# Weights that are loaded as they lie in HBM and turned by DMA transposes, in a cross-attention and ternary-FFN kernel

## The chip, the cores and the metric

The kernel runs on one core of a Trainium2 chip. The metric is the device time of one execution in microseconds (us). The core has TensorE (PE in the profile; its weight loads are PEld), VectorE (DVE), ScalarE (ACT), GpSimd (POOL) and SyncE (SP), which issues nearly all DMAs here. PEclk is the TensorE clock that the throttle granted.

## The reference

There are B = 4 sequences of L = 512 rows, D = 512, context width C = 256, head width H = 128, hidden width F = 2048.

```python
query = ctx @ Wq.T + bq;  key = ctx @ Wk.T + bk          # ctx (4,512,256) -> (4,512,128)
attention = softmax(query @ key.T)                       # (4,512,512)
x = x + layernorm(x) @ attention
scale = max(mean(|w|), 1e-8); wq = clip(round(w / scale), -1, 1)   # for w1 (2048,512) and w2 (512,2048)
x = x + gelu(layernorm(x) @ w1q.T + b1) @ w2q.T + b2
```

The scale of a weight matrix is the mean of its absolute values. So no weight can be rounded until the whole matrix has been loaded and summed, and w1 must be rounded before the first hidden matmul, w2 before the first output matmul.

## The kernel before

All operands of the large matmuls are f16. Activations are carried as a high and a low f16 half, ternary weights are exact in f16. P = 128, NT = ND = 4 tiles of rows or of D, NF = 16 tiles of F, NCH = 8 chunks of 1024 columns per weight matrix.

**Order of the work.** Every engine has its own hand-written program, and semaphores tie them. Per sequence b there are: projection and scores (f32), exponentials, `attend` (layernormed x times attention, 4 tiles of 12 matmuls), the second layernorm, `hidden(b, g)` (4 groups of 32 matmuls), `output(b, t)` (4 tiles of 32 matmuls). PE does attend(0) and attend(1) first, then hidden(0, 0) to hidden(0, 3) with the projection of sequence 2 before the last, scores of sequence 2, and output(0, 0) to output(0, 3). From then on FFN and attention of later sequences alternate.

**The weights.** SP loads each weight matrix in two halves, a half in four DMAs of 512 KB, each to 32 partitions (`load_w`, L257), so that four 32-row blocks of a matrix's transpose lie in the four partition groups. ACT sums the absolute values chunk by chunk (`sum_abs`, L688), the last two chunks of w2 are summed by DVE (L837). PE's `total` (L470) adds over partitions, and DVE makes the scale and its inverse (`quantiser_scale`, L850). POOL multiplies and rounds each chunk in two instructions (`round_weights`, L393: L397 and L400). DVE clips (L886) and transposes 32x32 blocks of pairs of f16 as u32 (L893) into `w1T` or `w2T`. PE waits for `turned_done`, one per chunk.

**The interleaving by pairs.** Since u32 pairs are turned, feature order inside a tile is permuted: `w1T[..., s]` is read with a stride of 2, results are written through `e_rows` and `e_columns`, and POOL writes `x2n` (L375) in blocks of 32.

**x2T, the layernormed x of the FFN.** For sequence 0 its tiles 0 and 1, and then 2 and 3, are normalised by POOL (`layernorm2`, L356), split in a high half by ACT (L671) and a low half by DVE (L783), staged in `gT_lo`, and turned by four DMA transposes of 128x1024 f16 (`turn_first_x2`, L274). They stand in SP's queue behind 12 of the 16 weight loads. hidden(0, 0) waits for all four. Later sequences use DMA transposes of 128x2048 f16.

**Buffers.** `w2T` lies over the lower half of `w1_raw`, the stages of later sequences over the upper half and over `w2_raw`.

The functions that the diff touches, and what calls them:

## Time and profile before

| | us |
|---|---|
| median of 3 runs | 320.81 (319.93 to 322.96) |
| the profiled execution | 320.93 |
| its span | 319.1 |
| PE busy | 304.6 |
| DVE / ACT / POOL busy | 166.8 / 144.0 / 117.4 |

Read the slices first: the busy share of PE in 40 slices of 8 us shows where it was not full. Then read the chain of work that ended last in order of time, which says from which moment on nothing but PE counts, and the timelines of the engines ahead of that moment. The mean of one f16 matmul of 512 columns is shown as about 380 ns, but matmuls are pipelined: 32 of them take 6.91 us in the chain, 0.216 us each. Idle time of an engine other than PE costs nothing by itself.

### The profile page before, as it was taken

The numbers are of one execution on the slowest core, as the hardware profiler recorded it, in microseconds if no ns is written. First come the engines' busy times: TensorE is split into PE (matmuls) and PEld (weight loads), VectorE is DVE, ScalarE is ACT, GpSimd is POOL, SyncE is SP. The second block draws the span as 40 slices with busy tenths as digits, with TensorE's granted clock in tenths as the row PEclk, the third lists the DMA queues.
The fourth block names the chain that finished last, engine by engine and source line by source line (L and its number), as shares of the span: only waits on it lengthen the run. The fifth ranks groups of instructions, "written<-read, shape, count | busy, mean of one in ns | idle before, by whom it ended". The sixth has DMA issues, their size and how long they took to land.

```text
span 319.1 us, 3686 instructions
## 1 busy us (share of the span) xinstructions
PE 304.6 (95%) x1397; PEld 143.7 (45%) x1397; DVE 166.8 (52%) x295; ACT 144.0 (45%) x251; POOL 117.4 (37%) x129
## 2 busy tenths in 40 slices
PE   7999979969987999999999999999999999999995
PEld 3465534434433444444444444444444444444455
DVE  2788868898689881754425630553424103342101
ACT  2287776686450652455374332456350006772000
POOL 0385369938998993000460560000470000000000
PEclk9999999999999999999999999999999999999999
DMA  8999999992100499000003947000016110000011
GB/s 198 271 209 211 213 137 219 214 278 68 31 0 0 87 175 267 0 2 0 0 0 69 174 89 199 0 0 0 2 31 130 39 66 0 0 2 0 33 62 40
DMA packets 57922, 28.04 MB, mean 88 GB/s; under 512 B 42800, under 2 KB 51760, under 8 KB 57904
## 3 DMA queue, kind: packets, MB, share of 16 engines
q1 hardware_dynamic: 57536, 27.53, 40.9%
q10 hardware_dynamic: 368, 0.27, 0.3%
q8 instruction: 11, 0.18, 0.2%
q14 instruction: 7, 0.06, 0.1%
HBM read 15.21 MB, written 4.19 MB: 61 GB/s over the span
## 4 chain that ended last, share of the span: by engine, by line
PE 73%; DMA 8%; SPq 8%; DVE 6%; ACT 3%; issue 2%
PE ps_e L526 31%; PE ps_t L509 29%; DMA w_raw<-in_L_ffn_w 7%; PE ps_e L494 6%; SPq L260 6%; PE ps_e L435 2%; PE ps_e L533 2%; PE ps_e L443 2%; ACT abs_out L695 1%; DVE tern L886 1%; DMA ctx_sb<-in_ctx 1%; SPq L277 1%; SPq L252 1%; DVE gT_lo L899 1%; DVE ctxT L763 1%
## 5 line engine op out<-in xcount | busy, mean ns | idle before, releaser
L509 PE MATMUL ps_t<-x2T,w1T 128*128 128x512 f16 x512 | 112.5, 379 | 0.0
L526 PE MATMUL ps_e<-w_raw,gT_hi 128*128 128x512 f16 x240 | 91.1, 380 | 3.0 <-DVE w_raw L893 3.0
L526 PE MATMUL ps_e<-w_raw,gT_lo 128*128 128x512 f16 x240 | 91.1, 380 | 0.0
L703 ACT ACTIVATE ps_t<-ps_t,b_col 128x512 f32<-128x512 f32 x64 | 42.2, 663 | 94.4 <-PE ps_t L509 94.4
L899 DVE SCALAR_TENSOR_TENSOR gT_lo<-ps_t,h_scale,gT_hi 128x512 f16<-128x512 f32 x64 | 44.9, 743 | 64.6 <-ACT gT_hi L708 64.6
L509 PEld LDWEIGHTS ps_t<-x2T,w1T 128*128 128x128 f16 x512 | 50.1, 98 | 60.6 <-issue 0.7
L905 DVE SCALAR_TENSOR_TENSOR x_sb<-ps_e,h_unscale,x_sb 128x512 f32<-128x512 f32 x15 | 11.2, 747 | 57.5 <-PE ps_e L526 57.5
L708 ACT ACTIVATE gT_hi<-ps_t,h_scale 128x512 f16<-128x512 f32 x64 | 40.3, 685 | 0.0
L526 PEld LDWEIGHTS ps_e<-w_raw,gT_hi 128*128 128x128 f16 x240 | 23.4, 98 | 33.1 <-DVE w_raw L893 4.5
L526 PEld LDWEIGHTS ps_e<-w_raw,gT_lo 128*128 128x128 f16 x240 | 23.5, 98 | 29.0 <-issue 1.7
L363 POOL TENSOR_SCALAR var_eps<-mv 128x4 f32<-128x4 f32 (+1 forms) x5 | 1.0, 196 | 81.4 <-DVE mv L835 81.4
L400 POOL TENSOR_SCALAR w_raw<-w_raw 128x1024 f16<-128x1024 f32 x16 | 22.0, 1378 | 1.4
L651 ACT ACTIVATE probs<-ps_e,row_max 128x512 f32<-128x512 f32 x16 | 10.9, 686 | 25.9 <-DVE row_max L803 25.7
L397 POOL TENSOR_SCALAR w_raw<-w_raw,inv_scale 128x1024 f32<-128x1024 f32 x16 | 19.5, 1218 | 6.3 <-DVE inv_scale L855 6.3
L494 PE MATMUL ps_e<-w_raw 128*128 128x512 f16 x96 | 21.7, 380 | 0.0
L391 POOL TENSOR_TENSOR x_sb<-x_sb,b_sb 128x512 f32<-128x512 f32 x16 | 21.2, 1357 | 0.0
L383 POOL TENSOR_SCALAR probs<-probs,row_inv 128x512 f32<-128x512 f32 x16 | 14.7, 935 | 15.6 <-DVE row_inv L808 15.6
L695 ACT ACTIVATE abs_out<-w_raw 128x1024 uint8<-128x1024 f32 x14 | 14.9, 1061 | 5.5 <-DMA w_raw<-in_L_ffn_w 5.2
L443 PE MATMUL ps_e<-qkT 128*128 128x512 f32 x32 | 14.8, 596 | 0.7 <-ACT qkT L645 0.7
L353 POOL TENSOR_SCALAR xn<-x_sb,neg_mean,rstd 128x512 f32<-128x512 f32 x16 | 14.9, 945 | 0.4
L494 PEld LDWEIGHTS ps_e<-w_raw 128*128 128x128 f16 x96 | 9.4, 98 | 11.3
L886 DVE TENSOR_SCALAR tern<-w_raw 128x1024 f16<-128x1024 f16 x16 | 14.1, 879 | 0.6 <-POOL w_raw L400 0.6
(90 smaller groups left out, 276.6 us busy)
## 6 DMA issues: line engine op xcount, KB each, us to landing
w_raw<-in_L_ffn_w SPq DMA_DIRECT2D x16, 512.0 KB, 10.0
x_sb<-in_x SPq DMA_DIRECT2D x4, 1024.0 KB, 8.2
out<-x_sb SPq DMA_DIRECT2D x15, 256.0 KB, 2.5
ctx_sb<-in_ctx SPq DMA_DIRECT2D x16, 128.0 KB, 3.4
b_sb<-in_L_ffn_b SPq DMA_DIRECT2D x1, 256.0 KB, 8.6
out<-x_sb SPq DMA_DIRECT2D x2, 128.0 KB, 2.3
x2n<-in_L_xattn_Wq ACTq DMA_DIRECT2D x1, 128.0 KB, 2.9
x2n<-in_L_xattn_Wk ACTq DMA_DIRECT2D x1, 128.0 KB, 3.8
```

The lines of the kernel that those rows point to most:

```text
L260: sp.dma_start(raws[m][q * R:(q + 1) * R, h * n:(h + 1) * n, :], w_views[m][q, :, h * n:(h + 1) * n, :]).then_inc(w_here[m][h], 16)
L391: nc.gpsimd.tensor_tensor(x_sb[:, b, t], x_sb[:, b, t], b2_sb[:], ALU.add).then_inc(b2_added, 1)
L397: nc.gpsimd.tensor_scalar(src, src, inv_scale[:, m:m + 1], ROUND, ALU.mult, ALU.add).then_inc(scaled, 1)
L400: nc.gpsimd.tensor_scalar(chunk_whole(m, c).rearrange("p n (i s) -> p n s i", s=2), src, -ROUND, 1.0, ALU.add, ALU.mult).then_inc(rounded, 1)
L443: nc.tensor.matmul(attn_bank(b, t)[:], qkT[:, 0, t * P:(t + 1) * P], qkT[:, 1], start=True, stop=True).then_inc(scores_ready, 1)
L494: mm = nc.tensor.matmul(attn_bank(b, t)[:], xnT(b)[:, u, j, t * P:(t + 1) * P], probsT(b)[:, v, j], start=(n == 0 and j == 0), stop=(n == ...
L509: mm = nc.tensor.matmul(ps_t[t][:], w1T[:, k // 2, j, :, k % 2], x2T[:, b % 2, v, :, j], start=(v == 0 and j == 0), stop=(v == 1 and j == ...
L526: mm = nc.tensor.matmul(y_bank(t)[:], part[:, k, t * P:(t + 1) * P], w2T[:, k], start=(k == 0 and part is gT_hi), stop=(k == NF - 1 and pa ...
L695: nc.scalar.activation(abs_out[:], flat[:, c * CH:(c + 1) * CH], ACT.Abs, accum_out=abs_sum[:, m, c:c + 1]).then_inc(abs_done, 1)
L703: nc.scalar.activation(ps_t[t][:], ps_t[t][:], ACT.Gelu, scale=1.0 / LN_SCALE, bias=b1_col[:, k:k + 1]).then_inc(gelu_done, 1)
L708: nc.scalar.activation(gT_hi[:, k], ps_t[t][:], ACT.Identity, scale=h_scale[:, 0:1]).then_inc(gT_hi_done, 1)
L899: nc.vector.scalar_tensor_tensor(out=gT_lo[:, k], in0=ps_t[t][:], scalar=h_scale[:, 0:1], in1=gT_hi[:, k], op0=ALU.mult, op1=ALU.subtract) ...
```

## The change

1. **Loads.** Each weight matrix is loaded over 128 partitions in four DMAs of 1 MB, w1 as 128 partitions x 4 rows of 512 (rows of 2 KB), w2 as 128 rows of 2048 (8 KB). SP issues all 16 loads (w2's second half, the context of sequence 2, b2, x of sequences 2 and 3 too) ahead of the first transposes.
2. **Turning.** DVE only clips. w1 is clipped in place and turned by eight DMA transposes of 128x1024 f16 (`turn_w1`). w2's chunks are clipped into `w2_ternary`, four chunks of room over the upper half of `w1_raw`, and turned two at a time by four DMA transposes of 128x2048 (`turn_w2`). All stand in SP's queue, turn_w1(0) between the two pairs of x2T. PE waits for `w1T_here[c]` and `w2T_here[n]`. The first clip of w2 waits until w1's chunks 4 to 7 have been turned, its fifth and seventh for the first and second turn of w2.
3. **Order.** All absolute sums go to ACT, earlier; the w1 total moves ahead of attend(1) on PE and on DVE, the w2 total from behind hidden(0, 1) to behind hidden(0, 0). The small layernorm steps (variance plus epsilon, minus mean) move from POOL to DVE, as does the normalisation of tiles 2 and 3 of sequence 0. POOL starts rounding w1 before it makes the `rstd2` that this needs.
4. **Plain order.** The pair interleaving goes, with `e_rows`, `e_columns` and the blocked write of x2n.

The core of the diff (what is left out renames semaphores, warms up on another tile, and makes views plain):

```diff
-        w1_raw = sb("w1_raw", [P, F // R, P])
-        w2_raw = sb("w2_raw", [P, D // R, F // Q])
-        w1T = sb("w1T", [P, NF // 2, ND, P, 2], F16)
+        w1_raw = sb("w1_raw", [P, NF, D])
+        w2_raw = sb("w2_raw", [P, ND, F])
+        w1T = sb("w1T", [P, NF, ND, P], F16)
...
-        tern = sb("tern", [P, 2, CH], F16)
...
+        w2_ternary = w1_stage[:, 0].rearrange("p v m -> p (v m)").rearrange("p (n c) -> p n c", c=CH)
+        N_TERNARY = 4
...
         def chunk_source(m, c):
 
             if m == 0:
-                return w1_raw[:].rearrange("p (q k) e -> p q k e", q=Q)[:, :, 2 * c:2 * c + 2]
-            return w2_raw[:, :, 2 * R * c:2 * R * (c + 1)].rearrange("p (s h) i -> p h s i", s=2)
+                return w1_flat[:, c * CH:(c + 1) * CH]
+            return w2_raw[:, :, 2 * P * c:2 * P * (c + 1)]
 
         def chunk_whole(m, c):
 
-            return chunk_source(m, c)[:, :, 0].bitcast(F16)
-
-        def chunk_turned(m, c):
+            src = chunk_source(m, c)
             if m == 0:
-                return w1T[:, c].rearrange("p j f s -> p (j f s)").bitcast(U32).rearrange(
-                    "p (j q r) -> p q j r", j=ND, q=Q)
-            return w2T[:, 2 * c:2 * c + 2].rearrange("p k e -> p (k e)").bitcast(U32).rearrange(
-                "p (k h r) -> p h k r", k=2, r=R)
+                return src.bitcast(F16)[:, 0:CH]
+            return src.bitcast(F16)[:, :, 0:2 * P]
...
-        w_views = [w1.rearrange("(fb r) (q d) -> q r fb d", r=R, q=Q), w2.rearrange("(eb r) (q f) -> q r eb f", r=R, q=Q)]
-        b1_view = b1.rearrange("(q k c) -> k q c", q=Q, k=NF)
+        w_views = [w1.rearrange("(k p) d -> p k d", p=P), w2.rearrange("(j p) f -> p j f", p=P)]
...
             def load_w(m, h):
-                n = raws[m].shape[1] // 2
-                for q in range(Q):
-                    sp.dma_start(raws[m][q * R:(q + 1) * R, h * n:(h + 1) * n, :],
-                                 w_views[m][q, :, h * n:(h + 1) * n, :]).then_inc(w_here[m][h], 16)
+                n = raws[m].shape[1] // 4
+                for i in (2 * h, 2 * h + 1):
+                    sp.dma_start(raws[m][:, i * n:(i + 1) * n, :], w_views[m][:, i * n:(i + 1) * n, :]).then_inc(w_here[m][h], 16)
...
+            def turn_w1(c):
+                sp.wait_ge(tern_done, c + 1)
+                sp.dma_start_transpose(w1T[:, 2 * c:2 * c + 2].rearrange("p k j f -> p (k j) f"),
+                                       chunk_whole(0, c)).then_inc(w1T_here[c], 16)
+
+            def turn_w2(n):
+
+                if n == 0:
+                    for i in range(NCH // 2):
+                        sp.wait_ge(w1T_here[i], 16)
+                sp.wait_ge(tern_done, NCH + 2 * n + 2)
+                first = 2 * n % N_TERNARY
+                sp.dma_start_transpose(w2T[:, 4 * n:4 * n + 4].rearrange("p k (j e) -> p (k j) e", j=ND),
+                                       w2_ternary[:, first:first + 2].rearrange("p n c -> p (n c)")).then_inc(w2T_here[n], 16)
...
             load_w(0, 0)
             load_w(0, 1)
             load_w(1, 0)
-            turn_first_x2(0)
-            turn_first_x2(1)
             load_w(1, 1)
             load_ctx(2)
             sp.dma_start(b2_sb[:], b2.rearrange("(a d) -> a d", a=1).to_broadcast([P, D])).then_inc(b2_here, 16)
             load_x(2)
             load_x(3)
+            turn_first_x2(0)
+            turn_w1(0)
+            turn_first_x2(1)
+            for c in range(1, NCH):
+                turn_w1(c)
             load_ctx(3)
+            for n in range(NCH // 2):
+                turn_w2(n)
...
-            def inverse_std(b, mv_t, ready, ve, nm, step_done, r, r_done, used):
-                pool.wait_ge(ready, NT * b + NT)
-                if b:
-                    pool.wait_ge(used, NT * b)
-                nc.gpsimd.tensor_scalar(ve[:], mv_t[:, :, 1], LN_EPS, LN_SCALE ** -2, ALU.add, ALU.mult).then_inc(step_done, 1)
-                nc.gpsimd.tensor_scalar(nm[:], mv_t[:, :, 0], -1.0, None, ALU.mult).then_inc(step_done, 1)
-                pool.wait_ge(step_done, 2 * b + 2)
-                nc.gpsimd.tensor_tensor(r[:], ve[:], minus_half[:], ALU.pow).then_inc(r_done, 1)
-                pool.wait_ge(r_done, b + 1)
+            def inverse_std(c, ve, r, step, n, done):
+
+                pool.wait_ge(step, 2 * n + 2)
+                nc.gpsimd.tensor_tensor(r[:, c], ve[:, c], minus_half[:, c], ALU.pow).then_inc(done, 1)
+                pool.wait_ge(done, n + 1)
...
-                    nc.gpsimd.tensor_scalar(x2n[:, t].rearrange("p (j q c) -> p q j c", j=ND, q=Q),
-                                            x_sb[:, b, t].rearrange("p (q j c) -> p q j c", q=Q, j=ND),
-                                            neg_mean2[:, t:t + 1], rstd2[:, t:t + 1],
+                    nc.gpsimd.tensor_scalar(x2n[:, t], x_sb[:, b, t], neg_mean2[:, t:t + 1], rstd2[:, t:t + 1],
...
+                    if m == 0 and c == 0:
+
+                        inverse_std(slice(2, NT), var_eps2, rstd2, ln2_step, 1, rstd2_done)
                     pool.wait_ge(scaled, NCH * m + c + 1)
-                    nc.gpsimd.tensor_scalar(chunk_whole(m, c).rearrange("p n (i s) -> p n s i", s=2), src, -ROUND, 1.0,
-                                            ALU.add, ALU.mult).then_inc(rounded, 1)
+                    nc.gpsimd.tensor_scalar(chunk_whole(m, c), src, -ROUND, 1.0, ALU.add,
+                                            ALU.mult).then_inc(rounded, 1)
...
-            layernorm2(0, range(2, NT), 1)
...
-                        pe.wait_ge(turned_done, 2 * g + t // 2 + 1)
+                        pe.wait_ge(w1T_here[2 * g + t // 2], 16)
+                    if b == 0 and g == 0 and t == 3:
+                        pe.wait_ge(total_read, W1 + 1)
...
-                            mm = nc.tensor.matmul(ps_t[t][:], w1T[:, k // 2, j, :, k % 2], x2T[:, b % 2, v, :, j],
+                            mm = nc.tensor.matmul(ps_t[t][:], w1T[:, k, j], x2T[:, b % 2, v, :, j],
...
-                    if b == 0 and t == 0 and k % 2 == 0:
-                        pe.wait_ge(turned_done, NCH + k // 2 + 1)
+                    if b == 0 and t == 0 and k % 4 == 0:
+                        pe.wait_ge(w2T_here[k // 4], 16)
...
-            attend(1, lambda t: pe.wait_ge(x2_done, t + 1), [0])
-            pe.wait_ge(x2_done, NT)
-            total(W1, ps_e[3])
-
-            def free(t):
-                if t < 3:
-                    pe.wait_ge(x2_done, t + 1)
-                else:
-                    pe.wait_ge(total_read, W1 + 1)
-            attend(1, free, range(1, NT))
+            pe.wait_ge(bank_read[3], N_PROBS1 + 1)
+            total(W1, ps_t[3])
+            attend(1, lambda t: pe.wait_ge(x2_done, t + 1), range(NT))
 
             hidden(0, 0)
-            hidden(0, 1)
             pe.wait_ge(x2_done, 2 * NT)
             total(W2, ps_e[3])
+            hidden(0, 1)
             hidden(0, 2)
...
             high_turned_probs(0)
+            sum_abs(0, (0, 1))
             exps(1)
             high_turned_xn(1)
-            sum_abs(0, range(4))
+            sum_abs(0, (2, 3, 4, 5))
             high_turned_probs(1)
-            sum_abs(0, (4, 5))
+            sum_abs(0, (6, 7))
             high_x2(0, (0, 1))
-            sum_abs(0, (6, 7))
+            sum_abs(1, (0, 1, 2))
             high_x2(0, (2, 3))
-            sum_abs(1, range(4))
+            sum_abs(1, range(3, NCH))
...
-            sum_abs(1, range(4, NCH - ABS_BY_DVE))
...
+            def scaled_moments(c, mv_t, ve, nm, step):
+                nc.vector.tensor_scalar(ve[:, c], mv_t[:, c, 1], LN_EPS, LN_SCALE ** -2, ALU.add, ALU.mult).then_inc(step, 1)
+                nc.vector.tensor_scalar(nm[:, c], mv_t[:, c, 0], -1.0, None, ALU.mult).then_inc(step, 1)
...
+            def normalise_x2(tiles):
+
+                dve.wait_ge(rstd2_done, 2)
+                for t in tiles:
+                    nc.vector.tensor_scalar(x2n[:, t], x_sb[:, 0, t], neg_mean2[:, t:t + 1], rstd2[:, t:t + 1],
+                                            ALU.add, ALU.mult).then_inc(x2n_done, 1)
...
-                t_out = tern[:, n % 2]
                 dve.wait_ge(rounded, n + 1)
-                if n >= 2:
-                    dve.wait_ge(turned_done, n - 1)
                 whole = chunk_whole(m, c)
-                nc.vector.tensor_scalar(t_out.rearrange("p (n i) -> p n i", n=whole.shape[1]), whole, -1.0, 1.0, ALU.max,
-                                        ALU.min).then_inc(tern_done, 1)
-                dve.wait_ge(tern_done, n + 1)
                 if m == 0:
-                    flat = t_out.bitcast(U32).rearrange("p (q j c) -> p q j c", q=Q, c=R)
+                    out_t, in_t = whole, whole
                 else:
-                    flat = t_out.bitcast(U32).rearrange("p (h k c) -> p h k c", k=2, c=R)
-                nc.vector.transpose(chunk_turned(m, c), flat).then_inc(turned_done, 1)
+                    if c == 0:
+                        for i in range(NCH // 2, NCH):
+                            dve.wait_ge(w1T_here[i], 16)
+                    if c >= N_TERNARY:
+                        dve.wait_ge(w2T_here[(c - N_TERNARY) // 2], 16)
+                    out_t = w2_ternary[:, c % N_TERNARY].rearrange("p (k j f) -> p k j f", k=2, j=ND)
+                    in_t = whole.rearrange("p j (k f) -> p k j f", k=2)
+                nc.vector.tensor_scalar(out_t, in_t, -1.0, 1.0, ALU.max, ALU.min).then_inc(tern_done, 1)
...
-                nc.vector.scalar_tensor_tensor(out=e_rows(x_sb[:, b, t]), in0=e_columns(y_bank(t)[:]),
-                                               scalar=h_unscale[:, 0:1], in1=e_rows(x_sb[:, b, t]),
+                nc.vector.scalar_tensor_tensor(out=x_sb[:, b, t], in0=y_bank(t)[:],
+                                               scalar=h_unscale[:, 0:1], in1=x_sb[:, b, t],
...
+            abs_rows(W1)
             residual(0, 3)
             moments2(0, 3)
             aggregate2(0, (2, 3))
+            quantiser_scale(W1, ps_t[3])
             low_x2(0, (0, 1))
-            abs_rows(W1)
+            normalise_x2((2, 3))
+            quantise(0, 0)
+            low_x2(0, (2, 3))
             residual(1, 0)
-            quantiser_scale(W1)
-            low_x2(0, (2, 3))
             residual(1, 1)
-            quantise(0, 0)
+            turn_ctx(2)
+            quantise(0, 1)
             residual(1, 2)
-            quantise(0, 1)
-            residual(1, 3)
             quantise(0, 2)
             moments2(1, 0)
-
+            residual(1, 3)
             quantise(0, 3)
+            moments2(1, 1)
+            abs_rows(W2)
+            quantise(0, 4)
             low_gelus(0, (0, 1))
-            quantise(0, 4)
+            quantise(0, 5)
             low_gelus(0, (2, 3))
-            abs_sums()
-            quantise(0, 5)
+            quantiser_scale(W2, ps_e[3])
+            quantise(0, 6)
             low_gelus(0, (4, 5))
-            abs_rows(W2)
+            quantise(0, 7)
```

SP's queue from its first weight load. The rows of the kernel before (gT_lo is the stage of x2T, w_raw are the weights):

```order
L260 DMA w_raw<-in_L_ffn_w 32x32x128 x8
L260 DMA w_raw<-in_L_ffn_w 32x8x512 x4
L277 DMA_TRANSPOSE x2T<-gT_lo 128x8x128 [waits x2_hi_done]
L277 DMA_TRANSPOSE x2T<-gT_lo 128x8x128 [waits x2_lo_done]
L277 DMA_TRANSPOSE x2T<-gT_lo 128x8x128 [waits x2_hi_done]
L277 DMA_TRANSPOSE x2T<-gT_lo 128x8x128 [waits x2_lo_done]
L260 DMA w_raw<-in_L_ffn_w 32x8x512 x4
```

The same place after the change:

```order
L251 DMA w_raw<-in_L_ffn_w 128x4x512 x4
L251 DMA w_raw<-in_L_ffn_w 128x2048 x4
L243 DMA ctx_sb<-in_ctx 32x16x64 [waits ctxT_ready]
L243 DMA ctx_sb<-in_ctx 32x16x64 x3
L315 DMA b_sb<-in_L_ffn_b 128x512
L246 DMA x_sb<-in_x 128x4x512 x2
L267 DMA_TRANSPOSE x2T<-gT_lo 128x8x128 [waits x2_hi_done]
L267 DMA_TRANSPOSE x2T<-gT_lo 128x8x128 [waits x2_lo_done]
L286 DMA_TRANSPOSE w1T<-w_raw 128x8x128 [waits tern_done]
L267 DMA_TRANSPOSE x2T<-gT_lo 128x8x128 [waits x2_hi_done]
L267 DMA_TRANSPOSE x2T<-gT_lo 128x8x128 [waits x2_lo_done]
L286 DMA_TRANSPOSE w1T<-w_raw 128x8x128 [waits tern_done] x7
```

The x2T transposes now have all loads ahead of them, and the second pair has one of w1 ahead of it, which waits for DVE's first clip.

DVE between the second moments of sequence 0 and its low halves, before (L848 and L852 make the w1 scale, L783 the low halves, L822 the residual sums):

```order
L835 BN_AGGR mv2<-stats2 128x2 [waits stats2_done] x2
L783 TENSOR_TENSOR gT_lo<-x2n,gT_lo 128x4x128 [waits x2_hi_done] x2
L848 TENSOR_REDUCE abs_row<-abs_sum 128x1 [waits abs_done]
L822 SCALAR_TENSOR_TENSOR x_sb<-ps_e0,x_sb 128x512 [waits attn_ready]
L852 TENSOR_SCALAR scale<-ps_e3 128x1 [waits total_ready]
L855 RECIPROCAL inv_scale<-scale 128x1 [waits total_read]
```

The same place after the change:

```order
L834 BN_AGGR mv2<-stats2 128x2 [waits stats2_done] x2
L806 TENSOR_SCALAR var_eps2<-mv2 128x2 [waits mv2_done]
L807 TENSOR_SCALAR neg_mean2<-mv2 128x2
L854 TENSOR_SCALAR scale<-ps_t3 128x1 [waits total_ready]
L857 RECIPROCAL inv_scale<-scale 128x1 [waits total_read]
L778 TENSOR_TENSOR gT_lo<-x2n,gT_lo 128x4x128 [waits x2_hi_done] x2
L845 TENSOR_SCALAR x2n<-x_sb,neg_mean2,rstd2 128x512 [waits rstd2_done]
L845 TENSOR_SCALAR x2n<-x_sb,neg_mean2,rstd2 128x512
L895 TENSOR_SCALAR w1_raw<-w1_raw 128x1024 [waits rounded]
L778 TENSOR_TENSOR gT_lo<-x2n,gT_lo 128x4x128 [waits x2_hi_done] x2
```

The scale now comes ahead of the low halves, and the low halves of tiles 2 and 3 come behind their normalisation and the first clip, all on DVE.

DVE where w1 ends and w2 begins, after the change (L901 frees a PSUM bank of the hidden matmuls, L895 clips):

```order
L901 SCALAR_TENSOR_TENSOR gT_lo<-ps_t1,h_scale,gT_hi 128x512 [waits gT_hi_done]
L895 TENSOR_SCALAR w1_raw<-w1_raw 128x1024 [waits rounded]
L895 TENSOR_SCALAR w1_raw<-w2_raw 128x1024 [waits w1T_here6,w1T_here5,w1T_here7,w1T_here4,rounded]
L901 SCALAR_TENSOR_TENSOR gT_lo<-ps_t2,h_scale,gT_hi 128x512 [waits gT_hi_done]
L901 SCALAR_TENSOR_TENSOR gT_lo<-ps_t3,h_scale,gT_hi 128x512 [waits gT_hi_done]
```

The first clip of w2 waits for the DMA transpose of what the clip just ahead of it wrote, and two bank-freeing instructions stand behind it.

## Rows read from the trace of the kernel before

**Rows 1.** The page: the slices (8 us each).
```profile
PE   7999979969987999999999999999999999999995
...
PEclk9999999999999999999999999999999999999999
```

**Rows 2.** Chain that ended last: start us, us, what.
```profile
101.78 20.72 PE ps_e L526 x96
122.50 6.91 PE ps_t L509 x32
```

**Rows 3.** PE's timeline: start us, us, group [idle before <-releaser].
```profile
39.98 2.75 PE L494 MATMUL ps_e<-gT_hi 128*128 128x512 f16 x12
45.04 0.35 PE L473 MATMUL ps_e<-abs_row,ones 128*128 128x1 f32 x2 [2.30 <-DVE abs_row L848]
45.25 7.93 PE L494 MATMUL ps_e<-gT_hi 128*128 128x512 f16 x36
53.02 13.98 PE L509 MATMUL ps_t<-x2T,w1T 128*128 128x512 f16 x64
69.52 0.35 PE L473 MATMUL ps_e<-abs_row,ones 128*128 128x1 f32 x2 [2.52 <-DVE abs_row L848]
...
77.30 3.70 PE L435 MATMUL ps_e<-ctxT,WT 128*128 128x512 f32 x8 [0.50 <-DVE ctxT L763]
```

**Rows 4.** Waits: us in total, times, longest.
```profile
PE ps_e L526 <- DVE w_raw L893: 3.0, 3, 1.6
```

**Rows 5.** PE's timeline about the last of these waits.
```profile
97.05 0.38 PE L526 MATMUL ps_e<-w_raw,gT_lo 128*128 128x512 f16 x1
99.02 0.39 PE L526 MATMUL ps_e<-w_raw,gT_hi 128*128 128x512 f16 x1 [1.60 <-DVE w_raw L893]
```

**Rows 6.** Stretches: us, busy of each engine, PEclk, DMA share, GB/s (last column).
```profile
28.00:32.00 4.00, 4.00 (x21) 1.78 (x19) 2.92 (x9) 4.00 (x10) 2.27 (x4) 1.00 1.19 210
...
69.00:70.00 1.00, 0.48 (x4) 0.39 (x5) 0.38 (x2) 1.00 (x3) 0.00 (x0) 1.00 1.04 406
```

**Rows 7.** The transposes of the first x2T (L277): issue ns, issue to landing.
```profile
L277 SPq DMA_TRANSPOSE x2T<-gT_lo x4: 1308/1340/3961, 42.5 to 49.2; - x4
...
DMA to landing us min/median/max: 3.4/5.0/6.6
```

**Rows 8.** ACT's timeline: the absolute sums (L695) and copies of w1's time.
```profile
35.47 2.02 ACT L657 CAST gT_hi<-ps_t 128x512 f16<-128x512 f32 x4
39.11 1.06 ACT L695 ACTIVATE abs_out<-w_raw 128x1024 uint8<-128x1024 f32 x1 [1.61 <-DMA w_raw<-in_L_ffn_w]
```

**Rows 9.** DVE's timeline: moments, low halves, clips beside POOL and alone.
```profile
41.52 0.30 DVE L835 BATCH_NORM_AGGREGATE mv<-stats 128x2 f32<-128x6 f32 x2
45.70 1.27 DVE L783 TENSOR_TENSOR gT_lo<-x2n,gT_lo 128x512 f16<-128x512 f32 x2
49.35 1.31 DVE L886 TENSOR_SCALAR tern<-w_raw 128x1024 f16<-128x1024 f16 x1 [0.61 <-POOL w_raw L400]
71.39 0.42 DVE L886 TENSOR_SCALAR tern<-w_raw 128x1024 f16<-128x1024 f16 x1
```

**Rows 10.** POOL's timeline: pow of rstd2 (L367), x2n, the first chunks.
```profile
42.84 1.01 POOL L367 TENSOR_TENSOR rstd<-var_eps,minus_half 128x2 f32<-128x2 f32 x1
43.96 1.52 POOL L375 TENSOR_SCALAR x2n<-x_sb,neg_mean,rstd 128x512 f32<-128x512 f32 x2
45.89 2.00 POOL L397 TENSOR_SCALAR w_raw<-w_raw,inv_scale 128x1024 f32<-128x1024 f32 x1 [0.40 <-DVE inv_scale L855]
47.97 1.35 POOL L400 TENSOR_SCALAR w_raw<-w_raw 128x1024 f16<-128x1024 f32 x1
49.26 1.11 POOL L397 TENSOR_SCALAR w_raw<-w_raw,inv_scale 128x1024 f32<-128x1024 f32 x1
```

**Rows 11.** Page, the low halves of gelu: xcount | busy, mean ns of one | idle before.
```profile
L899 DVE SCALAR_TENSOR_TENSOR gT_lo<-ps_t,h_scale,gT_hi 128x512 f16<-128x512 f32 x64 | 44.9, 743 | 64.6 <-ACT gT_hi L708 64.6
```

**Rows 12.** PE's timeline at the start.
```profile
1.17 4.45 PE L540 MATMUL ps_e<-tern 128*128 128x512 f16 x10 [1.17 <-DVE tern L909]
```

117 lines of the change are left out of this document (50 added, 67 removed).

## The prediction

> **What bounds the kernel now.** I read the slices first, then the end of the chain, then the timelines before it. The slices show PE full to nine tenths or more from the 14th to the 39th of 40, and its clock full throughout [rows 1]. The chain that ended last has nothing but PE in it from 101.78 on, and its units are fixed: 32 f16 matmuls in 6.91 us, 96 in 20.72 [rows 2]. Behind that moment the change moves nothing that PE waits for: what it takes from DVE and POOL there was hidden. So the question is when PE starts hidden(1, 0), at 122.50 [rows 2]. Ahead of it the timeline shows three idle places that the weights cause: 2.30 us for the w1 total, 2.52 for the w2 total and 0.50 for the context [rows 3]. The waits add 3.0 us in output(0, 0) for the turning of w2 [rows 4]. A wait costs a little more than its idle time: from 97.05 to 99.02 are 1.97 us, of which 1.60 are idle and 0.22 the matmul's own beat, so about 0.15 is the restart [rows 5].
>
> The sum is made against the profiled execution, 320.93 us (span 319.1); the median of 320.81 lies 0.12 below.
>
> **Loads.** The weights now come at 210 GB/s, over 32 partitions at a time; a 128-partition load of the same row form as the new w1 loads came at 406 [rows 6]. Taken as 400, the 14.4 MB that stand before the first x2T transpose in SP's queue (both weights, two contexts, four x, counted from the shapes) are 36 us of transfer; the first ones are small and slower, and I take them to be in by about 42 us. That matters, for the first old transpose took 3961 ns to issue where the others took 1308 to 1340, and it was the one behind loads still on their way [rows 7]. The point where this binds is worked out in rival C. The trace has 210 against 406 for 32 and 128 partitions; the Trainium skill, "SBUF — State Buffer", Door 1, says why: partitions 0 to 31 reach half of the DMA ports, so the trace agrees. The same page sets HBM at about 358 GB/s for a core; the 406 lies over it, so I go by the row. By the page's figure the loads would be in some 3 us later (an estimate), and the first x2T transposes would be held until then.
>
> **The w1 total.** ACT had the last two sums waiting 1.61 us for data [rows 8]. With the data there earlier, and two sums taken into the idle time before the exponentials, the last sum (1.06 each, about 0.2 to read it out) ends near 39.9; before, it began at 39.11 with another behind it. PE's total then stands at 40.2 instead of 45.04, behind attend(0), and the 2.30 of idle before it goes. attend(1) is four tiles of 2.6 [rows 3], so PE has done with it at about 50.7; it was 53.02. Taken alone this is worth 2.3 us.
>
> **What hidden(0, 0) waits for.** It needs all four x2T transposes. The chain to the fourth, step by step:
> - DVE has the moments' aggregates at 41.8 as before [rows 9]. The variance and mean steps now on DVE and the scale with its reciprocal take four small instructions, about 0.6. POOL starts rounding at 42.55, against 45.89 [rows 10].
> - The first rounding step takes 2.0 as it did beside DVE's low halves [rows 10], then pow 1.0 [rows 10]: `rstd2` of tiles 2 and 3 at 45.8. Before, pow ended at 43.85, since it came ahead of the rounding. Here the change makes the x2 path 2 us later.
> - Normalisation of two tiles: POOL took 1.52 for two [rows 10]. On DVE, beside POOL's second step (1.35 [rows 10]), I bound each by 0.42, the clip alone, and 1.31, the clip beside POOL [rows 9], and take the upper end, since the neighbour is the same: done at about 48.4. The upper end is what the rows show of DVE and POOL together: 1.31 against 0.42. The Trainium skill, "SBUF — State Buffer", Who interferes with whom, has it that DVE in a two-port mode and GpSimd exclude each other for a whole instruction; it speaks against this move, and the sum holds it already.
> - The first clip stands between on DVE: it is done at 49.8 (0.42 to 1.31, upper end). Then the low halves of tiles 2 and 3, 1.27 for two [rows 9] and up to 2.0 beside POOL, end at 51.3 to 52.
> - SP: transposes 1 and 2 are issued long before; turn_w1(0) needs the clip, 1.3 to issue [rows 7], so SP is at it from 49.8 to 51.1. Then high (1.3), and the low one from about 52.5. From its issue to its landing the rows give 3.4 at the least, 5.0 in the middle and 6.6 [rows 7]; the two longer ones belong to transposes behind loads or behind others, so I take 3.4. x2T is whole at 55.9.
>
> So PE stands idle from 50.7 to 55.9, 5.2 us, and hidden(0, 0) starts 2.9 us later than before (53.02 [rows 3]). The gain at the total is all used up, and more.
>
> **From hidden(0, 0) to hidden(1, 0).** Before, 69.48 us. The following goes:
> - The w2 total moves up behind hidden(0, 0), and all sums are on ACT with early data: 2.52 and a restart, −2.7.
> - The context of sequence 2 is loaded and turned long before: −0.5. DVE's turning (1.2 us) lies in the idle stretch after the x2 path.
> - w2T: PE needed a chunk at each two of 16 tiles [rows 4]. Now POOL starts w2 at about H+10 (H is the start of hidden(0, 0)), at one chunk each 2.5 us (1.11 and 1.35 [rows 10]): eight are done at 86. The last turning of two chunks is through by about 92, and output(0, 0) asks for it at 95.7. So −3.0 and three restarts, −3.5, with a margin of 3.5 us as cover.
>
> One wait comes in. DVE's first clip of w2 writes where w1's chunks 4 to 7 lie, and waits for the turning of chunk 7, which it has itself clipped just ahead. Queued behind it are the low halves that free PSUM banks 2 and 3 of the third hidden group. Clip 7 is at H+14.3, the landing at H+17.8 (3.4 again), clip, and low half of 0.74 [rows 11], with the bank free at H+19.0. PE wants it at H+17.4, after two and a half groups of 6.91. That is +1.6 and a restart, +1.8.
>
> Sum of this stretch: −2.7 − 0.5 − 3.5 + 1.8 = −4.9.
>
> **Behind it** the plain row forms save at most 0.1 in the last residual. The warm-up and the first 30 us: nothing, PE is bound by projections there and by x, which came at a similar rate before.
>
> Total: +2.9 − 4.9 − 0.1 = −2.1, so 318.8. Bounds: with every DVE step at its low end and no wait at the clip of w2, hidden(0, 0) starts at 54.3 and the sum is −5; with the landing at its high end it comes to +4.7, which is rival F.
>
> **Rivals.**
> - B, the clock. PE ran its first 10 matmuls of 512 columns in 4.45 us, 0.44 each, the 1.2 GHz level; 0.216 is the 2.4 GHz one [rows 12, 2]. The longest idle time after that, 2.52 us, was followed by full clock [rows 1, 3]. The 5.2 us that I forecast is twice as long, so the rows don't exclude that the clock falls. If it does and comes back as at the start, about 12 matmuls run at 0.43 instead of 0.22: 2.6 us, giving 321.4. Against it is only that the idle may be shorter than I work out. The Trainium skill, "TensorE: Matmul & The Clock Gate", Part 1, states that an idle array is put back to the lower level; whether this stretch is enough no row shows.
> - D, faster. DVE's steps don't meet POOL's, the clip of w2 waits for little: 316.5, from the low bounds above with half the stall.
> - C, the loads. It decides when the loads are in after 47, since four transposes then no longer land by 55.9: 14.4 MB from the second microsecond on in 45 us is 320 GB/s over the whole time. At 290 they end at 51.7 and the transposes behind them put hidden(0, 0) at 60 or later: 323 and up; at the old 210 it would be over 10 us more. For it: the weight loads never ran faster than about 210, and w2's rows of 8 KB have no row at all. Against it: 406 in the same queue [rows 6].
> - F, slower, with its place at the w1 transposes. They read 1024-column chunks in place, and eight follow each other. If each lands 5.0 to 6.6 us after issue [rows 7], the fourth x2T transpose, which stands behind turn_w1(0), lands 3.2 later, and so does chunk 7 at the w2 clip: +6.4 at the worst, 322 to 325.2. It is slower than before from a landing of about 4.5 us on.
> - The change might not do what it says: were weights hidden anyway, removing their waits would move nothing. The 8.3 us of idle time with the weights as releasers speak against it.
>
> **How the numbers follow.** My forecast has 0.36, B 0.25, D 0.15, C 0.09, F 0.10, and 0.05 is left for what I don't see. The time is that of the forecast, 318.8. The range from 316.2 to 325.2 holds the forecast, B, D and F, about 0.85, less what spills over at its ends. A measurement of this kernel can tell about 1% (3.2 us) from no change: faster means below 317.6, slower above 324.0. Faster gets D and a little of the forecast, 0.21; slower C, half of F and part of the rest, 0.18; the remainder, 0.61, is no change.
>
> **What would show it.** In the profile after: the w1 total on PE at about 40 with no idle before it; attend(1) over at 51; idle time before the first L509-type group of about 5 us, released by an x2T DMA; the granted clock there (a fall is B); a DMA rate of about 400 up to some 42 us (less is C); the span of transposes from issue to landing (3.4, or F); no idle at the w2 total and in output(0, 0); one idle of 1.6 in the third hidden group released by DVE; hidden(1, 0) at about 120.5 and from then on the same spacing. It would be wrong above all if the normalisation and the low halves on DVE take another time beside POOL than the rows for the clip say, or if transposes and loads share the queue in another way than the 3961 ns tell.

## The result and the profile after

| | before | after |
|---|---|---|
| median of 20 runs each, us | 321.61 (318.90 to 323.59) | 323.83 (321.02 to 325.69) |
| the profiled execution's span | 319.1 | 323.4 |
| mean granted clock of TensorE in it | 1.00 | 0.979 |

The ratio after to before is 1.0071, with a 95% interval of 1.0046 to 1.0095. The forecast was 0.9935, a gain; it was a small loss. A second measurement of the changed kernel beside the experiments gave 1.0028 (1.0000 to 1.0057).

The page's slices of the changed kernel answer to [rows 1]:

```profile
PE   5899997599899999999999999999999999999996
...
PEclk9699999699999999999999999999999999999999
```

PE is full from the 12th slice on, two earlier than before. New are the two 6 in the row of the clock: the second slice (8 to 16 us) and the eighth (57 to 65 us). Before, that row was 9 throughout. (The row reads 9 in the warm-up too, in all traces, though its matmuls take 0.4 us each; that level is known from their time alone.) The timeline of PE, to be held against [rows 3] and [rows 12], has both places:

```profile
1.17 3.83 PE L538 MATMUL ps_e<-gT_lo 128*128 128x512 f16 x10 [1.17 <-DVE gT_lo L911]
...
9.04 6.38 PE L431 MATMUL ps_e<-ctxT,WT 128*128 128x512 f32 x8 [2.42 <-DVE ctxT L758]
...
16.20 3.70 PE L439 MATMUL ps_e<-qkT 128*128 128x512 f32 x8 [0.66 <-ACT qkT L636]
...
43.97 0.35 PE L469 MATMUL ps_t<-abs_row,ones 128*128 128x1 f32 x2
44.19 10.52 PE L490 MATMUL ps_e<-gT_hi 128*128 128x512 f16 x48
60.51 9.62 PE L507 MATMUL ps_t<-x2T,w1T 128*128 128x512 f16 x32 [5.81 <-DMA x2T<-gT_lo]
69.97 0.28 PE L469 MATMUL ps_e<-abs_row,ones 128*128 128x1 f32 x2
70.11 10.52 PE L507 MATMUL ps_t<-x2T,w1T 128*128 128x512 f16 x48
82.25 3.61 PE L507 MATMUL ps_t<-x2T,w1T 128*128 128x512 f16 x16 [1.62 <-DVE gT_lo L901]
```

The three idle places of the weights are gone: no wait stands at the totals (43.97, 69.97) and none in output(0, 0). In their place are 5.81 us before hidden(0, 0), released by an x2T transpose, and 1.62 in the third group, released by DVE's low halves. The 32 matmuls at 60.51 take 9.62 us where the same work took half of 13.98 in [rows 3]. The windows of that stretch (start:end, length, busy time of PE, PEld, DVE, ACT and POOL, clock, DMA share, GB/s) say that it is the clock:

```profile
28.00:32.00 4.00, 4.00 (x23) 2.69 (x22) 3.96 (x9) 3.97 (x10) 1.45 (x3) 1.00 1.01 418
48.00:52.00 4.00, 4.00 (x21) 1.81 (x19) 2.89 (x3) 0.89 (x3) 3.82 (x5) 1.00 0.79 149
60.00:64.00 4.00, 3.49 (x9) 1.29 (x10) 3.06 (x6) 0.00 (x0) 3.91 (x4) 0.50 0.85 158
```

0.50 is the 1.2 GHz level. The first line shows the new loads at 418 GB/s where [rows 6] had 210. What sets the start of hidden(0, 0) is in the chain of waits (start, length, what):

```profile
46.41 2.00 POOL w_raw L391
48.41 0.67 POOL rstd L347
49.11 2.64 DVE x2n L845 x2
51.75 1.19 DVE w_raw L895
...
52.95 1.23 SPq L286
...
54.23 1.33 SPq L267
...
55.60 4.87 DMA x2T<-gT_lo
60.51 9.62 PE ps_t L507 x32
```

Rounding (L391), pow (L347), normalisation (L845), clip (L895), the issue of w1's transpose (L286), the issue of the high x2T (L267) and the landing of the low one stand one behind the other, as the forecast had them.

The difference of the two executions, 4.3 us, by stretches (starts from the timelines and the chains). Up to the scores of sequence 0: 12.23 became 16.20, +3.97; of this the first projection at the lower clock is 2.71 (6.38 for 3.67), and its later start (9.04 for 7.78) 1.26, since the first context landed at 7.63 and not at 6.36. From there to hidden(0, 0): 40.79 became 44.31, +3.52. From there to hidden(1, 0), at 122.50 and now 127.26: 69.48 became 66.75, −2.73. The rest: −0.5.

### The profile page after: what moved, and what is told of

Read it like the earlier page. It is cut to its first block, busy times and chain, and to the rows that moved or that the text cites. A ratio compares the mean times of both kernels' runs of the same rounds, so it can differ in the third digit from the quotient of the medians.

```text
span 323.4 us, 3660 instructions
## 1 busy us (share of the span) xinstructions
PE 308.3 (95%) x1397; PEld 145.4 (45%) x1397; DVE 162.9 (50%) x297; ACT 146.3 (45%) x255; POOL 106.4 (33%) x109
## 4 chain that ended last, share of the span: by engine, by line
PE 88%; DMA 4%; DVE 4%; SPq 1%; POOL 1%; ACT 1%; issue 0%; DVEq 0%
PE ps_t L507 33%; PE ps_e L524 32%; PE ps_e L490 10%; PE ps_e L439 4%; PE ps_e L431 4%; PE ps_e L531 2%; DMA ctx_sb<-in_ctx 2%; DMA x2T<-gT_lo 2%; PE ps_t L463 1%; PE ps_t L431 1%; DMA w1T<-w_raw 1%; DVE w_raw L895 1%; DVE x2n L845 1%; DVE gT_lo L901 1%; POOL w_raw L391 1%; PE ps_t L450 1%
## 5 line engine op out<-in xcount | busy, mean ns | idle before, releaser
L507 PE MATMUL ps_t<-x2T,w1T 128*128 128x512 f16 x512 | 115.1, 385 | 7.4 <-DMA x2T<-gT_lo 5.8
L901 DVE SCALAR_TENSOR_TENSOR gT_lo<-ps_t,h_scale,gT_hi 128x512 f16<-128x512 f32 x64 | 45.0, 745 | 66.7 <-ACT gT_hi L703 66.6
L347 POOL TENSOR_TENSOR rstd<-var_eps,minus_half 128x4 f32<-128x4 f32 (+1 forms) x9 | 8.5, 947 | 102.0 <-DVE neg_mean L807 102.0
L391 POOL TENSOR_SCALAR w_raw<-w_raw,inv_scale 128x1024 f32<-128x1024 f32 x16 | 20.8, 1297 | 10.7 <-DVE inv_scale L857 10.7
L895 DVE TENSOR_SCALAR w_raw<-w_raw 128x1024 f16<-128x1024 f16 x16 | 15.1, 954 | 6.7 <-DMA w_raw<-w_raw 3.3
L397 POOL TENSOR_SCALAR w_raw<-w_raw 128x1024 f16<-128x1024 f32 x16 | 17.3, 1079 | 1.4
L690 ACT ACTIVATE abs_out<-w_raw 128x1024 uint8<-128x1024 f32 x16 | 17.1, 1067 | 0.5
L431 PE MATMUL ps_e<-ctxT,WT 128*128 128x512 f32 x24 | 13.6, 719 | 2.4 <-DVE ctxT L758 2.4
```

The costliest lines, as they stand in the source:

```text
L391: nc.gpsimd.tensor_scalar(src, src, inv_scale[:, m:m + 1], ROUND, ALU.mult, ALU.add).then_inc(scaled, 1)
L397: nc.gpsimd.tensor_scalar(chunk_whole(m, c), src, -ROUND, 1.0, ALU.add, ALU.mult).then_inc(rounded, 1)
L431: mm = nc.tensor.matmul(qk_bank(b, s)[:], WT[:, s, k], ctxT[:, k], start=(k == 0), stop=(k == NC - 1))
L507: mm = nc.tensor.matmul(ps_t[t][:], w1T[:, k, j], x2T[:, b % 2, v, :, j], start=(v == 0 and j == 0), stop=(v == 1 and j == ND - 1))
L895: nc.vector.tensor_scalar(out_t, in_t, -1.0, 1.0, ALU.max, ALU.min).then_inc(tern_done, 1)
L901: nc.vector.scalar_tensor_tensor(out=gT_lo[:, k], in0=ps_t[t][:], scalar=h_scale[:, 0:1], in1=gT_hi[:, k], op0=ALU.mult, op1=ALU.subtract) ...
```

## The experiments

Kernels of one group ran on the same chip and share the runs of the kernel before. The first four experiments are one group, the control and the next three the second; the last two and "POOL normalises first, the rest as in the changed kernel" are the third. Ratios are to the kernel before, with their 95% intervals. The mean granted clock of a run tells how much of it was at the lower level. It takes steps: about 1.00, 0.995, 0.989, 0.984, 0.979.

**Fill the idle time before hidden(0, 0).**

```diff
             attend(1, lambda t: pe.wait_ge(x2_done, t + 1), range(NT))
+            for _ in range(22):
+                nc.tensor.matmul(ps_t[0][:], xnT(1)[:, 0, 0, 0:P], probsT(1)[:, 0, 0], start=True, stop=True)
             hidden(0, 0)
```

> 22 dummy matmuls of 512 columns (into bank ps_t0, on operands of attend(1)) stand on PE between attend(1) and hidden(0, 0) and fill most of the 5.8 us of idle time. Theory (the clock fell because of that idle time): the granted clock stays 1.00 between 56 and 68 us, hidden(0, 0) takes 7.0 instead of 9.6 us, the whole 2.6 us less than the changed kernel: ratio to the kernel before about 0.999. Rival (the slow matmuls are those of x2T or w1T still on the way, not the clock): hidden(0, 0) stays at 9.6 and the time at that of the changed kernel, 1.007.

0.9931 (0.9908 to 0.9954), 319.45 us. PE's timeline of that place:

```profile
53.88 4.91 PE L571 MATMUL ps_t<-gT_hi 128*128 128x512 f16 x22
58.63 7.07 PE L507 MATMUL ps_t<-x2T,w1T 128*128 128x512 f16 x32
```

4.75 us of useless work make the next group 2.55 us shorter. The idle time, not x2T or w1T, made it slow: that cause is shown. The ratio fell by 0.014, some 4.5 us, more than the 2.6 expected; against the second measurement of the changed kernel it fell by 0.010, 3.1 us. Not all of this is the clock. From the scores (15.55) to hidden(0, 0) are 43.08 us, 1.23 less than in the changed kernel, since the last x2T transpose landed 3.1 us from its issue and not 4.87. That landing has two lengths in the traces with this order of the queue (start, length, what; the second trace of the changed kernel, the next experiment, and the one that fills the start alone):

```profile
53.29 4.83 DMA x2T<-gT_lo
52.73 4.91 DMA x2T<-gT_lo
52.11 3.26 DMA x2T<-gT_lo
```

With POOL normalising first and the rest as it is it is 4.85, with both fills 3.2. What decides between the two was not found, and a single trace of each kernel can't tell whether the other runs of it are alike. So 2.55 us is the clock, and up to 1.6 us in the comparisons below can be this landing.

**The wait at w2's first clip.**

```diff
-            quantise(1, 0)
             low_gelus(0, (6, 7))
+            quantise(1, 0)
```

> On DVE the low halves of gelu tiles 6 and 7 go ahead of the first clip of w2, so they no longer stand behind its wait for w1's last transpose. Theory: the idle 1.6 us of PE in the third hidden group goes, with its restart 1.8: ratio to before about 1.001 to 1.002. Rival (the bank is freed late anyway, or w2's turning becomes late in output(0, 0)): PE's idle time only moves, ratio 1.007.

0.9977 (0.9951 to 1.0004). The groups two to four of hidden(0) and the projection run through:

```profile
57.69 8.82 PE L507 MATMUL ps_t<-x2T,w1T 128*128 128x512 f16 x32 [5.43 <-DMA x2T<-gT_lo]
66.35 0.28 PE L469 MATMUL ps_e<-abs_row,ones 128*128 128x1 f32 x2
66.49 13.97 PE L507 MATMUL ps_t<-x2T,w1T 128*128 128x512 f16 x64
80.30 3.60 PE L431 MATMUL ps_e<-ctxT,WT 128*128 128x512 f32 x8
```

The 1.62 are gone and nothing took their place; output(0, 0) has no wait either. Against the two measurements of the changed kernel the ratio fell by 0.005 and 0.009, 1.6 and 3.0 us, for 1.8 expected. The wait is shown to be gone; its worth in time isn't known better than that.

**Order of the first clip and the x2T path.**

```diff
             turn_first_x2(0)
-            turn_w1(0)
             turn_first_x2(1)
+            turn_w1(0)
...
-            quantise(0, 0)
             low_x2(0, (2, 3))
+            quantise(0, 0)
```

> The low halves of x2's tiles 2 and 3 go ahead of the first clip on DVE, and the second pair of x2T transposes ahead of w1's first one on SP. Theory (a serial chain norm, clip, low halves, w1 transpose, x2T transposes sets hidden(0, 0)): the clip (1.2) and the issue of w1's transpose (1.2) leave the x2T path, but w1's transpose now comes last, so hidden(0, 0) starts 1 to 2 us earlier; the idle time is still about 4 us and the clock may fall. Ratio about 1.002, or 0.995 where the clock stays. Rival (x2T's landing, 4.9 us, is bound by bandwidth of the transposes in flight): the start of hidden(0, 0) does not move, 1.007.

0.9940 (0.9916 to 0.9963). From the scores at 14.91 to hidden(0, 0) at 57.08 are 42.17 us where the changed kernel had 44.31. The chain ahead of it:

```profile
52.52 3.37 DMA x2T<-gT_lo
55.88 1.20 issue
57.08 8.45 PE ps_t L507 x32
```

x2T lands at 55.88, 40.97 us behind the scores instead of 44.27: its last transpose is issued 1.8 us earlier, and lands in 3.37 instead of 4.87. The last 1.2 us are w1's first chunk, which now comes last. The clock still falls (8.45).

**The same, and POOL normalises first** (`layernorm2(0, range(2, NT), 1)` ahead of `round_weights(0)`, without the pow inside it and without `normalise_x2`).

> As e3_swap, and POOL normalises tiles 2 and 3 of x2 before it starts rounding w1, as in the kernel before, so DVE has no normalisation. Theory (the late rstd2 and the normalisation beside POOL are what holds x2T back): x2n is there at 48.3 instead of 51.75 of the profile after, rounding starts 2 us later, hidden(0, 0) starts 3 to 4 us earlier than in the changed kernel, PE is idle for about 2 us, and the clock does not fall: 3.5 + 2.6 = 6 us less, ratio about 0.989. Rival (the first w1 chunk, now 2 us later, is what hidden(0, 0) waits for): gain of 1 to 2 us only, clock falls, ratio 1.002.

0.9908 (0.9881 to 0.9935), 318.71 us.

```profile
49.20 3.27 DMA x2T<-gT_lo
52.48 1.51 issue
53.98 8.75 PE ps_t L505 x32
```

From the scores (12.22) to hidden(0, 0) are 41.76 us: 2.5 less than in the changed kernel, not 3 to 4. x2T is there 1.5 us before PE starts: the rival holds for the last part, the first w1 chunk. And 3.27 us of idle time (PE's timeline) are still followed by the lower clock, against what I expected.

**POOL normalises first, the rest as in the changed kernel.**

> POOL normalises tiles 2 and 3 before it starts rounding, as in the kernel before, and DVE and SP keep the order of the changed kernel (clip and w1's transpose ahead of the second pair). Theory (the place of w1's first chunk in the chain is what counts, since rounding now starts 2 us later): hidden(0, 0) starts 0 to 1 us earlier than in the changed kernel, clock falls stay, ratio 1.001 to 1.007. Rival (the normalisation on DVE beside POOL, 2.64 us, is the whole delay): 2.6 us earlier, ratio 0.995.

0.9984 (0.9955 to 1.0012). From the scores (12.04) to hidden(0, 0) (55.98) are 43.94 us, 0.4 less than in the changed kernel. So the normalisation on DVE, 2.64 us for two tiles, was not by itself what counted. Nor was the place of the first clip: it ends at 47.62, 35.6 us behind the scores, where the changed kernel had 36.7 (52.92). But SP, which issues the first pair of x2T transposes while loads are still landing, is at the second of them for 3.17 us, up to 48.31. Only then does it issue w1's transpose, and the second pair stands behind that. The last landing, 4.85 us, is of the long kind. Turning the order round alone brought hidden(0, 0) 2.1 us forward, of which 1.5 is the shorter landing; the two edits together brought 2.5.

**A control.** The changed kernel again, in one group with the next three.

> The changed kernel as it is, as a control beside the next three. Ratio to the kernel before 1.007 as first measured; mean granted clock of its runs 0.979 to 0.989, with a slow stretch at the start of hidden(0, 0) in every one of them. If the ratio comes out at 1.00 here, the differences of the first four experiments must be read against that.

1.0028 (1.0000 to 1.0057). Its twelve runs have clocks of 0.984 in eight, 0.989 in three and 0.995 in one. Twenty-nine runs of the kernel before in the same group: 0.998 to 1.00 in seven, 0.993 to 0.995 in sixteen, 0.984 to 0.989 in six. The first trace of before, at 1.00, was thus of the rarer kind.

**The width of the weight loads.**

```diff
-                for i in (2 * h, 2 * h + 1):
-                    sp.dma_start(raws[m][:, i * n:(i + 1) * n, :], w_views[m][:, i * n:(i + 1) * n, :])...
+                for q in range(Q):
+                    sp.dma_start(raws[m][q * R:(q + 1) * R, h * n:(h + 1) * n, :],
+                                 w_views[m][q * R:(q + 1) * R, h * n:(h + 1) * n, :])...
```

> The weights are loaded in their natural order, but each DMA takes 32 partitions (512 KB) instead of all 128 (1 MB). Theory (rival C of the prediction, the number of partitions sets the rate): about 210 GB/s while the weights come instead of 400, so they are in at about 55 us and the x and context loads behind them at about 60; the first x2T transposes stand behind all of them in SP's queue and hidden(0, 0) starts 7 us later or more: ratio 1.03 or above. Rival (rows of 2 KB and 8 KB rather than 512 bytes make the rate): 350 to 400 GB/s, the time of the changed kernel, 1.007.

1.0488 (1.0432 to 1.0543), 337.06 us. A window of the loads, and PE's timeline (in this view, cut off at 80 us, the last row shows 14 of 32 matmuls):

```profile
28.00:36.00 8.00, 5.17 (x31) 3.05 (x30) 3.80 (x10) 6.03 (x15) 2.69 (x4) 1.00 1.09 233
```

```profile
47.52 0.35 PE L470 MATMUL ps_t<-abs_row,ones 128*128 128x1 f32 x2 [2.25 <-DVE abs_row L851]
47.73 12.21 PE L491 MATMUL ps_e<-gT_hi 128*128 128x512 f16 x48
74.52 5.77 PE L508 MATMUL ps_t<-x2T,w1T 128*128 128x512 f16 x14 [14.58 <-DMA x2T<-gT_lo]
```

The rows lie in HBM as in the changed kernel and the bytes are the same, but the rate is 233 instead of 418 GB/s. Rows of 2 KB and 8 KB don't make the rate. What is left is the partitions that one DMA reaches, and its size, 512 KB and not 1 MB, which changes along with them; 128 partitions at 512 KB were not tried. The transposes behind the loads come late: hidden(0, 0) starts at 74.52, 60.2 us behind the scores (14.34) instead of 44.3, twice the shift expected. This is rival C, made real. The Trainium skill, "SBUF — State Buffer", Door 1, has the rate of a DMA hang on how many of the DMA ports its partitions reach. The 233 and 418 GB/s agree with it.

**The start of both kernels.**

```diff
+            for _ in range(8):
+                nc.tensor.matmul(ps_e[0][:], gT_lo[:, 0, 0:P], gT_lo[:, 0], start=True, stop=True)
             pe.wait_ge(WT_done, 1)
             project(0, lambda s: None)
```

> Eight dummy matmuls of 512 columns stand ahead of the first projection, in PE's idle time at 6.6 us while it waits for the context. Theory (a clock fall between 8 and 14 us comes in most runs of both kernels from that idle time): the first projection takes 3.7 us in nearly all runs, mean granted clock one step higher (0.989 to 0.995), 2 to 2.5 us less than the changed kernel: ratio 0.999. Rival (the slow first projection is a matter of the f32 matmuls or of what is loaded then): no change of the clock, 0 to 1.5 us more than the changed kernel, for the matmuls that then delay the projection.

> The same eight dummy matmuls in the kernel before. Theory (the start is a matter of both kernels, and no part of the change): the mean granted clock of its runs goes from mostly 0.995 to 1.00 and the time falls by 1 to 2 us: ratio 0.995. Rival (only the changed kernel falls at the start): no change but the delay, ratio 1.00 to 1.004.

In the changed kernel: 0.9949 (0.9917 to 0.9982), 2.5 us less than the control beside it. Its timeline:

```profile
6.60 1.90 PE L550 MATMUL ps_e<-gT_lo 128*128 128x512 f16 x8
8.33 3.60 PE L431 MATMUL ps_e<-ctxT,WT 128*128 128x512 f32 x8
...
55.41 9.75 PE L507 MATMUL ps_t<-x2T,w1T 128*128 128x512 f16 x32 [4.21 <-DMA x2T<-gT_lo]
```

The first projection takes 3.60 us where it had 6.38, and 5.37 in the control's trace; the fall at hidden(0, 0) stays. The two traces of this group differ by 2.3 us: 1.2 up to the scores, 1.6 from there to hidden(0, 0), where the last x2T transpose lands in 3.26 instead of 4.83, and −0.4 in hidden(0, 0) itself (9.75 for 9.31). In the kernel before: 0.9995 (0.9960 to 1.0030), no change. Seven of its twelve runs still show 0.994 or 0.995, so its fall in those runs lies elsewhere, or comes in spite of the fill; no trace of such a run was taken. The expectation for the kernel before failed. That the fill keeps the clock up in the first projection of the changed kernel is shown; of the 2.5 us some 1.2 are seen there, and up to 1.6 can be the landing.

The changed kernel's start doesn't always fall. In the traces of kernels with that start and no fill the first projection took 5.25 to 6.71 us in five and 3.67 in three, of which two with nearly the same idle time ahead of it, first the control, then the experiment on the wait at w2's first clip:

```profile
1.17 4.05 PE L538 MATMUL ps_e<-gT_lo 128*128 128x512 f16 x10 [1.17 <-DVE gT_lo L911]
7.74 5.37 PE L431 MATMUL ps_e<-ctxT,WT 128*128 128x512 f32 x8 [1.50 <-DVE ctxT L758]
```

```profile
1.17 4.45 PE L538 MATMUL ps_e<-gT_lo 128*128 128x512 f16 x10 [1.17 <-DVE gT_lo L911]
8.20 3.67 PE L431 MATMUL ps_e<-ctxT,WT 128*128 128x512 f32 x8 [1.51 <-DVE ctxT L758]
```

In the five the ten warm-up matmuls took 3.68 to 4.36 us, in the three 4.45, as in the trace of the kernel before. In these traces the fall goes with how the warm-up went, and that differs between executions of one kernel (3.83 and 4.05 us in the two of the changed kernel). Whether the change makes it more frequent stays open: there is one unfilled trace of the kernel before.

**Both fills.**

> The changed kernel with both sets of dummy matmuls, 8 ahead of the first projection and 22 between attend(1) and hidden(0, 0). Nothing else is moved. Theory (the clock, and only the clock, turned the forecast gain into a loss): no stretch at half clock in most runs, mean granted clock 0.995 to 1.00, ratio 0.990, which is the forecast of 0.9935 without the falls that the kernel before has itself at the start. Rival (the two fills act through something else, such as the time at which loads and transposes meet, and don't add): ratio of e1_gap or of e6_start_after again, 0.993 to 0.995.

0.9897 (0.9872 to 0.9922), 318.63 us. All six runs have a clock of 1.00 and spans of 315.8 to 317.4: no fall is left in any of them. Against the control's 1.0028 the fills alone are worth 0.0097 and 0.0079, and both 0.0131, so the parts add for the most part, not in full. The groups ran on different chips, and the interval overlaps that of the first fill alone.

**All that the experiments point to.**

> All that the experiments point to: POOL normalises tiles 2 and 3 first, the low halves and the second pair of x2T transposes go ahead of the first clip and w1's first transpose, the low halves of gelu tiles 6 and 7 go ahead of w2's first clip, 12 dummy matmuls before hidden(0, 0) and 8 before the first projection. If the parts add: hidden(0, 0) 2.5 us earlier than in the changed kernel, 1.8 for the stall, against e8_fills: ratio 0.977 to 0.980. Rival (the parts meet in one bound, the first w1 chunk, or PE is then held by w2's turning in output(0, 0)): 0.985.

0.9805 (0.9776 to 0.9834), 315.52 us: 6 us faster than the kernel before, and so faster than both.

```profile
41.20 0.35 PE L467 MATMUL ps_t<-abs_row,ones 128*128 128x1 f32 x2 [0.54 <-DVE abs_row L852]
...
51.77 2.75 PE L571 MATMUL ps_t<-gT_hi 128*128 128x512 f16 x12
55.80 7.07 PE L505 MATMUL ps_t<-x2T,w1T 128*128 128x512 f16 x32 [1.28 <-issue]
```

It is 3 us better than both fills alone, not 4.3. What is left is named by these rows: 0.54 for the w1 total and 1.28 for the first w1 chunk, which lands at 55.71. Ahead of the total ACT's sums stand one behind the other without a wait for data, so it is the order of the work on ACT and DVE and no longer the loads. The 12 dummy matmuls fill only part of the gap; the 1.28 us of idle time behind them were followed by full clock (7.07).

## Why the prediction was wrong

Two steps failed: the clock at hidden(0, 0), taken as full, and the start, put at nothing ("The warm-up and the first 30 us: nothing"). The steps in the order of the prediction:

- **The w1 total**: right. 27.8 us behind the scores (43.97 − 16.20), as the forecast's 40.2 is 28.0 behind 12.23.
- **Loads**: right in rate (418 for 400) while the weights came, the last of which landed at 40.60. The rest came slower (228 and 203 GB/s from 36 to 40 and 40 to 44 us), and x of sequence 3 landed at 49.35, 45.4 on the old time scale, where all loads were to be in by 42. The weights still came early enough for every sum. x2T's first pair took 1.35 and 1.57 us to issue and 5.56 and 3.60 to land; the second pair didn't meet the loads. The list behind the 14.4 MB leaves out b2 and one of three contexts; the sum has them. The old transpose with 3961 ns was the second of the four, not the first. The estimate by 358 GB/s comes to some 4 us later (14.4 MB in 40.2 us for 36), not 3.
- **The x2T chain**: right in kind and in its steps. The normalisation took 2.64 for two tiles, the upper end taken (2 × 1.31 [rows 9]). The Trainium skill, "SBUF — State Buffer", Who interferes with whom, states that DVE in a two-port mode and GpSimd exclude each other for a whole instruction, and that `tensor_scalar` can enter such a mode. The trace fits it: the two normalisations end at 50.49 and 51.75, each 0.28 behind a POOL instruction that ran beside it; no run has them on DVE without POOL. The landing was undersized: 4.87 instead of 3.4. The same transpose in the same queue landed in 3.1 to 3.3 in three other traces, so the transposes ahead of it don't explain the length; the cause stays open. The issue was 0.9 sooner than forecast, so the start of hidden(0, 0) came 3.5 later than before, not 2.9.
- **From hidden(0, 0) to hidden(1, 0)**: the wait at w2's clip was forecast as 1.6 and is 1.62. The whole stretch changed by −2.73; with the 2.63 that the half clock adds to the first group (9.62 against 6.99) taken out, by −5.4, where −4.9 was forecast.
- **The clock**: this step failed, and cost 2.6 us in the trace. I put it down as rival B with 0.25 and made the forecast with a full clock, because 2.52 us of idle time were followed by full clock in the trace before. Idle times of 3.3, 3.7, 4.2, 4.8, 5.4, 5.5 and 5.8 us were followed by the lower level in every trace taken. The row of 2.52 had no say over one of 5.2, and nothing in the trace spoke for a full clock there. The Trainium skill, "TensorE: Matmul & The Clock Gate", Part 1, says that the array is put back to the lower level when idle. The traces agree with it at these seven idle times; rival B should have been the forecast.
- **The start and the baseline**: the second step that failed, and the larger one in the profiled execution. I made the sum against one execution with a clock of 1.00. Most runs of the kernel before lose something to the clock, so there was some to lose at the start as well. In the two profiled executions the scores came 3.97 later, 2.71 by the slower first projection and 1.26 by the first context. How much of it belongs to the change, and how much to the execution, isn't known; the control's trace has +1.66.

Rival B's own time was 321.4; the median came out at 323.83, the profiled execution at 325.17. The latter is accounted for: 321.4, +3.97 for the start, +0.6 for hidden(0, 0) later than forecast, −0.5 for the stretch behind it and −0.4 for the rest, which makes 325.1. So the clock at hidden(0, 0) was sized right by rival B (2.63 for 2.6), and what B lacked was the start. Two bounds of the prediction don't add up, without weight for the result: the low end gives −5.5, not −5, and F's 325.2 is +4.3, not +4.7.

That the forecast's mechanism was otherwise near complete is supported by both fills: with no fall anywhere, the spans have a median of 316.85 against 318.1 for the nine runs of the kernel before at a clock of 0.998 or more in the second and third group, −1.3 us where −2.1 was forecast. In that trace the last x2T transpose landed in 3.2 us, near the forecast's 3.4; with the longer landing the gain would be about 1.2 us smaller (an estimate: it would land at 56.7, where hidden(0, 0) began at 55.53), and next to nothing of it would be left. The experiment with the first fill alone gave 0.9931, the ratio of the forecast, but that is luck: its trace still has a first projection of 6.71 us, and it is held against runs of the kernel before that lose to the clock themselves.

## What to carry to other kernels

Before an edit is costed at "PE waits x longer", ask what PE does after the wait: the idle times of this case, 3.3 to 5.8 us, were each followed by a group that took 1.4 to 2.7 us longer, and useless matmuls in their place give that back. Waits removed in several places and put together in one can be a loss though the sum is smaller: 8.3 us before, 7.4 after (5.81 and 1.62). And one profiled execution may be of the lucky kind: look at the granted clocks of all runs of the kernel before summing against it. When two kernels differ by a microsecond or two, split their traces into the same stretches: here a landing that has two lengths stood beside the effect under test.
